# Block order, copies and row splits of the paired tiles in an attention and gate kernel

## The reference

```
xn = layernorm(x)
s  = attention(xn, Wq, Wk, Wv) @ Wo          # 16 heads of 64, causal, rotary
g  = silu((xn * in_scale) @ sign(W).T * out_scale + bias)
out = x + s * g
```

## Time and profile before

| | |
|---|---|
| median of 3 runs | 1165.83 us (1165.61 to 1166.93) |
| profiled execution | 1166.2 us, span in the trace 1164.4 us |
| PE busy | 1121.4 us, 96% of the span |
| DVE, ACT, POOL busy | 69%, 55%, 35% |
| granted TensorE clock, mean | 0.991 |

### The profile page before, as it was taken

The page is one execution under the profiler, slowest core; times in us unless marked ns, Lnnn a source line. Parts: engine busy times, 40 slices in busy tenths (PEclk is TensorE's granted clock), DMA queues, the critical chain, the costliest instruction groups (busy, mean ns, idle before and its releaser), DMA issues.

```text
span 1164.4 us, 17756 instructions
## 1 busy us (share of the span) xinstructions
PE 1121.4 (96%) x5620; PEld 932.8 (80%) x5620; DVE 799.3 (69%) x1848; ACT 641.8 (55%) x1350; POOL 410.2 (35%) x253
## 2 busy tenths in 40 slices
PE   4899999999999999999999999999999999979998
PEld 3577777788888888888888888888888887867776
DVE  6757741477767777677676776767767678887574
ACT  6545542266665666556665566656666577543331
POOL 0433537343342433425334252342523534630000
PEclk9899999999999999999999999999999999999999
DMA  9425132220202202022360220202202036665752
GB/s 370 191 91 235 55 91 109 73 64 10 63 9 72 63 9 63 9 72 63 147 213 9 72 63 9 63 9 72 63 9 63 9 111 223 212 242 169 244 172 109
DMA packets 88431, 116.30 MB, mean 100 GB/s; under 512 B 3536, under 2 KB 69072, under 8 KB 87376
## 3 DMA queue, kind: packets, MB, share of 16 engines
q1 hardware_dynamic: 88400, 115.91, 29.6%
HBM read 82.35 MB, written 33.55 MB: 100 GB/s over the span
## 4 chain that ended last, share of the span: by engine, by line
PE 79%; DVE 9%; DMA 4%; issue 2%; ACT 2%; POOL 2%; SPq 0%; POOLq 0%; DVEq 0%; ACTq 0%
PE at_proj L44 16%; PE at_proj L46 16%; PE at_proj L45 16%; PE at_out L1103 7%; PE ff_z_ps L287 6%; PE at_pt L1090 6%; PE at_score L1072 4%; PE at_score L1073 3%; DMA rope_table<-att_store 2%; POOL ff_xs_lo L679 1%; PE at_proj L1057 1%; DVE xs_full L600 1%; PE ff_tr L219 1%; DMA z<-fn_in_channel_scale_dram 1%; DMA z<-_attn_hidden_states_dram 1%
## 5 line engine op out<-in xcount | busy, mean ns | idle before, releaser
L44 PE MATMUL at_proj<-xn_hi,w_hi 128*128 128x512 f32 x824 | 333.6, 405 | 1.6 <-POOL w_lo L1756 0.8
L46 PE MATMUL at_proj<-xn_hi,w_lo 128*128 128x512 f32 x824 | 322.8, 392 | 0.0
L45 PE MATMUL at_proj<-xn_lo,w_hi 128*128 128x512 f32 x824 | 321.4, 390 | 0.0
L1740 POOL TENSOR_TENSOR at_turning<-at_turning,rope_table 128x512 f32<-128x512 f32 x64 | 83.0, 1298 | 289.3 <-DVE at_turning L1467 289.3
L46 PEld LDWEIGHTS at_proj<-xn_hi,w_lo 128*128 128x128 f32 x824 | 154.6, 188 | 34.5
L44 PEld LDWEIGHTS at_proj<-xn_hi,w_hi 128*128 128x128 f32 x824 | 155.0, 188 | 29.2 <-issue 1.2
L45 PEld LDWEIGHTS at_proj<-xn_lo,w_hi 128*128 128x128 f32 x824 | 155.3, 188 | 27.5
L1276 ACT ACTIVATE at_prob<-at_score,at_neg_max 128x512 f32<-128x512 f32 (+3 forms) x256 | 133.3, 525 | 71.1 <-DVE at_neg_max L1495 70.7
L1748 POOL TENSOR_TENSOR w_lo<-w_stage,w_hi 128x1024 fp32r<-128x1024 f32 x45 | 114.5, 2558 | 162.7 <-ACT w_hi L1238 162.7
L1285 ACT ACTIVATE at_pt_hi<-at_pt 128x512 fp32r<-128x512 f32 (+1 forms) x192 | 94.0, 524 | 100.0 <-PE at_pt L1090 99.2
L1512 DVE TENSOR_TENSOR at_pt_lo<-at_pt,at_pt_hi 128x512 fp32r<-128x512 f32 (+1 forms) x192 | 112.0, 597 | 42.3 <-ACT at_pt_hi L1285 41.3
(11 more groups left out here) (214 smaller groups left out, 1984.3 us busy)
## 6 DMA issues: line engine op xcount, KB each, us to landing
z_store<-z SPq DMA_DIRECT2D x16, 512.0 KB, 2.8
w_stage<-in_L_attn_Wq_dram SPq DMA_DIRECT2D x16, 512.0 KB, 3.8
w_stage<-in_L_attn_Wk_dram SPq DMA_DIRECT2D x16, 512.0 KB, 5.1
w_stage<-in_L_attn_Wv_dram SPq DMA_DIRECT2D x16, 512.0 KB, 6.1
att_store<-at_att_t SPq DMA_DIRECT2D x32, 256.0 KB, 2.0
rope_table<-att_store SPq DMA_DIRECT2D x16, 512.0 KB, 4.9
at_turning<-z_store SPq DMA_DIRECT2D x16, 512.0 KB, 5.3
w_stage<-_attn_hidden_states_dram SPq DMA_DIRECT2D x13, 512.0 KB, 6.4
```

The costliest lines, as they stand in the source:

```text
L44: pe.matmul(out, sh, mh, start=first, stop=False, skip_group_check=reopened)
L45: pe.matmul(out, sh, ml, start=False, stop=False, skip_group_check=reopened)
L46: return pe.matmul(out, sl, mh, start=False, stop=final, skip_group_check=reopened)
L1740: pool.tensor_tensor(swapped[c][:], swapped[c][:], rope[:, 2 * c + 1, :], ALU.mult).then_inc(rot_a, 1)
```

## The change

1. PE: the products of a pair go A11, S1, S2, S4, S3, A12, A22 where they went A11, A12, S1, S2, S3, S4, A22. The banks are then a, c, a, c, a, b, a; before: a, b, c, a, a, c, a. The copy of bank c is waited for before S4.
2. ACT: all three `part_copy` of a pair stand first in the round of the loop, then `silu`, the hi of A11 and S1 of the next pair, the second `silu`, and the other five hi. Before, they alternated.
3. DVE: `row_sums` of the next pair, the lo of A11 and of S1 come first in the round, then both early block sums; the lo of A12 comes after the block (0,0), which is now the last but one.
4. Pair 0: the hi and lo of A22 come directly behind those of A11 and A12 on ACT and POOL; the hi of S4 and S3 come ahead of `silu(3)`; `row_sums` forms S4 ahead of S3.
5. SP: `load_x(2)` is issued earlier, `load_att(7)` directly behind `load_att(6)`; in the loop `store_y(n)` and `load_z(n + 2)` come ahead of `load_att(n + 4)`, and `load_att(n + 5)` ahead of `load_z(n + 3)`.

```diff
             load_rows(2)
             load_att(5)
+            load_x(2)
             load_rows(3)
             store_y(1)
             load_z(3)
-            load_x(2)
             load_x(3)
             store_y(2)
             load_z(4)
             load_att(6)
+            load_att(7)
             load_x(4)
             load_x(5)
-            load_att(7)
 ...
             for n in range(PLAIN, TILES, 2):
-                if n + 4 < TILES:
-                    load_att(n + 4)
                 store_y(n)
                 if n + 2 < TILES:
                     load_z(n + 2)
+                if n + 4 < TILES:
+                    load_att(n + 4)
                 store_y(n + 1)
+                if n + 4 < TILES:
+                    load_att(n + 5)
                 if n + 2 < TILES:
                     load_z(n + 3)
                 if n + 4 < TILES:
-                    load_att(n + 5)
                     load_x(n + 4)
                     load_x(n + 5)
 ...
                 product(a, A11, wo_block(0, 0), True)
-                wait_row_low(pe, q, 2)
-                product(b, A12, wo_block(1, 0), True)
                 pe.wait_ge(op_low_dve, 4 * q + 1)
                 product(c, S1, wo_sum_block(T1), True, sum_low_dve if q == 0 else None)
 ...
                 product(a, S2, wo_sum_block(T2), False)
                 pe.wait_ge(op_low_dve, 4 * q + 3)
+                pe.wait_ge(partial_ok, 3 * q + 2)
+                product(c, S4, wo_block(1, 1), False)
+                pe.wait_ge(op_low_dve, 4 * q + 4)
                 pe.wait_ge(sum_low_pool, 2 * QT - 1)
                 pe.wait_ge(partial_ok, 3 * q + 3)
                 product(a, S3, wo_sum_block(T3), False)
-                pe.wait_ge(op_low_dve, 4 * q + 4)
-                product(c, S4, wo_block(1, 1), False)
+                wait_row_low(pe, q, 2)
+                product(b, A12, wo_block(1, 0), True)
                 wait_row_low(pe, q, 3)
 ...
             op_hi(0, A11)
             op_hi(0, A12)
+            op_hi(0, A22)
             sums_high(2)
             op_hi(0, S1)
             op_hi(0, S2)
             sums_high(3)
+            op_hi(0, S4)
+            op_hi(0, S3)
             silu(3, 1)
-            for op in (S3, S4, A22):
-                op_hi(0, op)
 ...
                 part_copy(q, 0)
+                part_copy(q, 2)
+                part_copy(q, 1)
+                silu(n, 0)
                 if more:
                     op_hi(q + 1, A11)
-                silu(n, 0)
-                if more:
-                    op_hi(q + 1, A12)
-                part_copy(q, 2)
-                if more:
                     op_hi(q + 1, S1)
-                part_copy(q, 1)
-                if more:
-                    op_hi(q + 1, S2)
                 silu(n + 1, 1)
                 if more:
-                    for op in (S3, S4, A22):
+                    for op in (S2, S4, S3, A12, A22):
                         op_hi(q + 1, op)
 ...
                 more = q + 1 < ROUNDS_W
-                block_sum(q, 0)
-                if more:
-                    row_low(q + 1, A11)
+                if more:
                     row_sums(q + 1, 0)
                     row_sums(q + 1, 1)
-                    row_low(q + 1, A12)
-                    op_low(q + 1, S1)
-                block_out(q, 0, 0, 0, False)
-                if more:
-                    op_low(q + 1, S2)
-                block_sum(q, 2)
-                if more:
-                    op_low(q + 1, S3)
-                block_out(q, 2, 1, 1, False)
-                block_sum(q, 1)
-                block_out(q, 1, 0, 1, True)
-                if more:
-                    op_low(q + 1, S4)
+                    row_low(q + 1, A11)
+                    op_low(q + 1, S1)
+                block_sum(q, 1)
+                block_sum(q, 2)
+                if more:
+                    op_low(q + 1, S2)
+                block_out(q, 1, 0, 1, False)
+                block_out(q, 2, 1, 1, False)
+                if more:
+                    op_low(q + 1, S4)
+                    op_low(q + 1, S3)
+                block_sum(q, 0)
+                block_out(q, 0, 0, 0, True)
+                if more:
+                    row_low(q + 1, A12)
                 block_21(q)
                 if more:
                     row_low(q + 1, A22)
 ...
             op_low(0, A11)
             op_low(0, A12)
+            op_low(0, A22)
             sums_low(2)
             sums_low(3)
-            op_low(0, A22)
```

More of the change, by code:

```diff
@@ L820, in attention_block @@
         ROUNDS_W = (TILES - PLAIN) // 2
-        A11, A12, S1, S2, S3, S4, A22 = range(7)
+        A11, S1, S2, S4, S3, A12, A22 = range(7)
         T1, T2, T3, T4 = range(4)
-        SUM_ORDER = (S1, S2, S3, S4)
+        SUM_ORDER = (S1, S2, S4, S3)
+        HIGH_ORDER = ((A11, A12, A22, S1, S2, S4, S3), (A11, S1, S2, S4, S3, A12, A22))
         def x_slot(n):
@@ L840, in operand @@
                 return [a22[:, part, :].rearrange("p (k n) -> p k n", k=QT) for part in range(2)]
-            pair, half = ((2, 0), (2, 1), (0, 0), (0, 1), (1, 0), (1, 1))[op]
+            pair, half = {A11: (2, 0), A12: (2, 1), S1: (0, 0), S2: (0, 1), S3: (1, 0), S4: (1, 1)}[op]
             return [w[pair][:, QT * half:QT * (half + 1), :] for w in (w_hi, w_lo)]
@@ L847, in att_rows, with high_count @@
             return att_raw[:, tile, half * HALF:(half + 1) * HALF]
+        def high_count(q, op):
+            return 7 * q + HIGH_ORDER[q > 0].index(op) + 1
         def flat(ap):
@@ L1401, in op_hi @@
                     act.wait_ge(product_done, 7 * (q - 1) + op + 1)
-                elif op in (S2, S1):
+                elif op in (S1, S2):
                     act.wait_ge(y_mm, PLAIN - 1)
@@ L1416, in part_copy @@
             def part_copy(q, which):
-                act.wait_ge(product_done, 7 * q + (1, 4, 3)[which])
+                act.wait_ge(product_done, 7 * q + (1, 3, 2)[which])
                 if q >= 1:
-                    act.wait_ge(block_done, 3 * (q - 1) + (1, 3, 2)[which])
+                    act.wait_ge(block_done, 3 * (q - 1) + (3, 1, 2)[which])
                 act.activation(partial[:, which, :], banks[q % 2][(0, 0, 2)[which]][:], ACT.Copy).then_inc(partial_ok, 1)
@@ L1614, in row_sums @@
                 a21, a22_raw = (att_raw[:, 1, h * HALF:(h + 1) * HALF] for h in range(2))
-                s1, s2, s3, s4 = (att_sum[:, i, :] for i in range(4))
+                s1, s2, s4, s3 = (att_sum[:, i, :] for i in range(4))
                 if part == 0:
@@ L1620, in row_sums @@
                 else:
-                    dve.tensor_tensor(s3, a11, a21, ALU.subtract).then_inc(att_sums, 1)
                     dve.wait_ge(att_sums, 4 * q + 2)
                     dve.tensor_tensor(s4, a12, s2, ALU.subtract).then_inc(att_sums, 1)
+                    dve.tensor_tensor(s3, a11, a21, ALU.subtract).then_inc(att_sums, 1)
             def op_low(q, op):
-                dve.wait_ge(op_high, 7 * q + op + 1)
+                dve.wait_ge(op_high, high_count(q, op))
                 hi, lo = operand(op)
@@ L1635, in block_sum @@
             def block_sum(q, which):
-                dve.wait_ge(product_done, 7 * q + (2, 6, 5)[which])
+                dve.wait_ge(product_done, 7 * q + (6, 4, 5)[which])
                 dve.wait_ge(partial_ok, 3 * q + (1, 3, 2)[which])
@@ L1646, in block_out @@
                 z, x = z_tile[:, p, cols], x_tile(n)[:, cols]
-                order = (0, 2, 1).index(which)
+                order = (1, 2, 0).index(which)
                 dve.wait_ge(block_read, 3 * q + order + 1)
@@ L1708, in _ @@
             row_sums(0, 1)
+            op_low(0, S4)
             op_low(0, S3)
-            op_low(0, S4)
             gate(3, 1)
@@ L1803, in op_low @@
             def op_low(q, op):
-                pool.wait_ge(op_high, 7 * q + op + 1)
+                pool.wait_ge(op_high, high_count(q, op))
                 hi, lo = operand(op)
```

## The result

The changed kernel is slower: 1169.56 us, median of 11 runs (1168.53 to 1172.02), against 1166.47 us of the kernel before in the same sessions (11 runs, 1162.78 to 1169.19). The ratio is 1.0026, 95% interval 1.0015 to 1.0038, +3.0 us by the ratio and 3.1 by the medians. I had forecast 1165.9 us, no change, with a range of 1160.0 to 1169.5, so the measured time lies just above its upper end. The mechanism was right, a loop through landing, DVE's work, store and burst; one of its terms, the burst, was too small.

What follows compares the result with a forecast made beforehand. The bound was taken to be a loop of landing, DVE work, store and burst. -2.0 us at pair 2's row sums, +4.6 in three periods, -3.7 + 1.2 in the last stretch gave +0.1: 1165.9 us, range 1160.0 to 1169.5.

Steps and rivals of the forecast that it cites:

- The bound: Output stage: a loop of landing, DVE's work, store and burst, 21.0 us a pair against PE's 19.04; copy wait a symptom.
- PE's order: New product order removes PE's 12.7 us of waits on copies; the product of A22, awaiting two block sums, is late next.
- DVE's order: Row sums first puts all work behind the landing; the tile's end and store release come 1.3 us later.
- X: Start of a pair's row sums on DVE, once its rows have landed; a number after it gives the pair.
- The burst: DMAs from issue of the store to the next row sums: 10.3 us before, 10.85 forecast, bounds 9.8 and 11.6.
- the upper bound: Burst of 11.6 us, if the z now behind the rows overtakes them as the x loads did.
- X2: Start of pair 2's row sums on DVE: forecast 1064.1 us (1062.0 to 1065.2), 2 us earlier than before.
- Pair 0: Its edits bring pair 1's row sums to 1040 us; PE idles 2.2 us before S2; most of the gain is lost later.
- The last stretch: From the start of pair 5's row sums to the end: 31.7 us plus 1.2 for the clock, before 35.45.
- The sum: Span 1164.5 us against 1164.4, +0.1 us, so a median of 1165.9 us.
- Rival 3: Slower, overtaken rows: z and x behind them take their share; period 23.3 or more, median 1169.1 us; chance 0.24.
- Rival 2: The loop lets go: landing at the best DMA rate, 8.2 us; period 19.9, median 1155 us; chance 0.06.

Runs made afterwards that it cites:

- new queue: Kernel before with only SP's loop put in the changed order; ratio 1.0058 to the kernel before.
- x held: Changed kernel with both loads of x in SP's loop held back until the odd rows have landed; 1170.56 us, ratio 1.0034 to the kernel before.
- z held: Changed kernel with the z and x loads queued behind the odd rows held until those landed; one execution, store issue to next row sums 11.2 us mean.
- half rows: Changed kernel with even tiles' row loads halved from tile 8 on; one execution, store issue to next row sums 10.2 us mean.
- stores last: Changed kernel with both stores in SP's loop moved behind the loads of z and rows; 1156.07 us, ratio 0.9910 to the kernel before.

## Why the prediction was wrong, step by step

*The bound.* Right: a loop, with the copy as its symptom. The runs with other queue orders moved the time by -13.5 to +6.8 us with no edit to any engine but SP.

*PE's order.* Right: the stands at copies went, the new ones are at A22's block sum.

*DVE's order.* X + 5.1 for the second block sum and X + 11.6 for the tile's end; measured 1070.94 + 0.68 - 1066.37 = 5.25, and 11.76. The step from S2 to S4 takes 0.82 us and not 0.72; the store follows at X + 11.79, where the period had 11.67.

*The burst: the step that failed.* I priced one z replaced by a load of rows at +0.5 us, from the busy share of a load that ran nearly alone, on the premise that the engines stay full, and took 10.85. It was 11.46 in the mean of the four bursts, 11.63 in the three that lie between X2 and X5. The engines did not stay full: two us at 147 GB/s in place of 333 are 1.1 us lost (an estimate, 2 x (1 - 147/333)), and the burst grew by 1.2. What I took for the upper bound, overtaking by what is behind, gave some 0.3.

Three periods were 2.7 us longer than forecast. Of these 0.4 are DVE's part (0.12 a period) and 2.3 the bursts, and 1.6 of the 2.3 are the third burst alone, by which it is longer than its neighbours (12.72 against 11.1). In the kernel before it is the longest as well, by 0.9, and in the runs with new queue, x held, z held and half rows by 0.8 to 1.3. So part of the miss is a size that I had spread over four bursts as a mean, and in this execution it was larger than in any other of these.

The Trainium skill, "DMA: Bandwidth & Descriptors", section "Specifications", gives 512 bytes as the least size of a transfer for line rate. The loads of rows are made of runs of just this size, and the trace agrees where their packets come densely: 321 GB/s in the microsecond with 579 short packets of 586, and 304 GB/s over three with the stores last. In the low stretch, at 147 GB/s, it is the number of packets that is low. The mechanism behind it is open: the long issue of z stood beside it, but holding z back left the low stretch in place, and two loads of rows one after the other did not bring it about.

*Pair 0.* Right within its bounds. X1 1039.8 (1040 forecast), PE's stand 2.65 us (2.2), X2 1064.8 (1064.1). Alone it gave -4.1 us.

*The last stretch.* Forecast 31.7 + 1.2 from X5 to the end, measured 33.6. A22 of pair 4 starts 5.4 us after X5 (5.3 forecast), so what is left for the clock is 1.7 and not 1.2: after the stand of 2.09 us the granted clock was 0.83 from 1140 to 1150.

*The sum.* Forecast +0.1; X2 +0.7, three periods +2.7, the last stretch +0.7: +4.2, which is what the profiled execution shows. The medians differ by 3.1. Break-even was a period of 22.5, where I put the forecast itself: with the whole result resting on a term that no row of before showed (rows early in the burst, with a store behind them), 0.24 for "slower" was too little, and the upper end too near.

*Rivals.* Rival 3, the slower one, came true by its numbers (period 23.3, median 1169.1) and not by its mechanism: the rows weren't overtaken, the engines carried them slowly for two us of each burst. That its time fits is luck. Rival 2, the loop that lets go, was the state that stores behind the loads bring about: a period of 19.6 and 1156 us measured, where the rival had 19.9 and 1155.

## What to carry to other kernels

Where several engines work ahead in step, look for the closed loop before pricing an edit: add up its parts from one landing to the next, compare it with the bound engine's own period, and ask what each reordering puts on it. In a burst of DMAs the order of issue is a schedule: loads for which the next step waits come first, each of those that the next step needs, and stores for which nobody waits come last; in the changed kernel that was worth 13.5 us of 1169.6, with its other orders as they were. An order of products that avoids waiting for a copy was worth just its 1.06 us a round, and only once the loop is shorter than that.

## What the runs showed of the hardware

- A load of 512 KB in runs of 512 bytes came at very different rates. With two of them one after the other and no store among them, three us of nearly only their packets moved 304 GB/s (1.04 busy). With a store directly behind one of them, two us moved 143 to 147 GB/s at 0.53 to 0.64 busy, in the changed kernel, in the kernel before with the changed queue, and in the changed kernel with the old queue, where only one such load is near. That the store is the cause is not shown.
- In its place in the changed queue such a load cost an estimated 2.5 us of a burst (half of it 1.27), where 512 KB at the mean rate of a burst, 333 GB/s, are 1.5.
- What was queued behind the odd rows, loads of z and x, delayed their landing by some 0.3 us or less (11.46 against 11.2 with nothing behind, one execution each).
- The DMA issued behind two such loads and a store took 3.4 to 3.7 us to issue on SP, against 0.43 for the like one at the head of the burst.
- Summing into a bank, copying it on ACT and summing into it again cost 1.06 us of PE's time, of which 0.57 is the copy; the same in ten instances of two kernels.
